# ScalarE takes ba's logits out of PSUM; block passes over 49 tiles; a folded prefix sum; one store moved

## The chip, the core and the metric

One core of a Trainium2 chip runs the whole program. Its engines are TensorE (PE; its weight loads are listed as PEld), VectorE (DVE), ScalarE (ACT), GpSimd (POOL) and SyncE (SP, which here only issues transfers). The metric is device time in microseconds (us), lower is better; the kernel before takes 11012.33 us, the median of three runs (11008.8 to 11015.49).

## What is computed

Four graph layers in a row over 6250 nodes of 128 features and 200000 edges. Cut to what matters here:

```python
# GCN: degree-normalised, weighted sum over edges
deg = segment_sum(w, dst) + 1
out = segment_sum((x @ W)[src] * norm[:, None], dst) + b
# gated graph network (2 rounds), then attention with 8 heads:
e = leaky_relu(s_i[row] + s_j[col], 0.2)
ex = exp(e - m[row])
denom = segment_sum(ex, row)                 # ba computes ex and denom
out = segment_sum(x_heads[row] * (ex / denom[row])[..., None], col)
# message passing layer, LayerNorm
```

## The kernel before

Nodes are laid out as 49 tiles of 128. The work is a row of stages, each a block with one instruction list per engine, coupled by semaphores; a barrier of all engines ends each stage. The stages that the change touches:

**prep** sorts the edges into a 49 x 49 grid of blocks (source tile by target tile), one slot per edge and at most 128 per block. Edges lie in groups of 14 x 128. A loop runs over 112 items (a group and a window of targets), two deep: GpSimd copies the item's fields, DVE makes the one-hot of the block (`OJ`), PE adds up prefix counts, DVE multiplies one-hot by prefix and reduces over 98 blocks to the edge's rank (L697 to L700), makes the one-hot of the rank (`OHr`), and PE places the records, which DVE adds into `X` (used as `RECS`). Before the loop DVE clears the buffers, `X` and `OJF` among them (L634 to L646), and then tells the others by `zeroed`. After the loop SyncE stores, in this order: `rec_d`, seven pieces of `gcn_d`, `dst2_d` (the list of edges that found no slot, by groups: `dst_d` in the trace's names), `dst2p_d` (the same by partitions), and `slot_d`, twice. `slot_d` is what the next stage reads.

**The GCN pass** (`block_pass("gcn")`) runs over target tiles, 50 of them (`NTP = NT + 1`; the last is padding, so that they go in pairs), each in 4 units of 12 or 13 blocks. SyncE loads a tile's slots (`rowsb`, two buffers), DVE makes a one-hot (L1195), PE gathers (L1267), DVE weighs (L1215) and makes the target's one-hot (L1202), PE adds (L1279), ACT copies the tile's sum out (L1254). `block_pass("heads")` does the same later, over the attention heads.

**ba** (`block_attention`) runs over 50 tiles as well, each in 3 units v of 17, 16 and 16 blocks (`AU`), two deep. In DVE's round for v stand: both one-hots of v (`hot`, L1892 and L1894); `second_rest` of v-2 (L1930); `logits` of v-1 (L1904 to L1909), which first copies PE's result `xp` from PSUM to `tx`; `source_hot` of v-1 (L1915); `first_rest` of v-1 (L1924). PE looks the logits of v up (L2012, L2015: six matmuls a block, `looks`), then adds the denominators of v-2 (L2026). ACT does, in order, `second_part` (L1973), exp (L1985), a cast (L1987), and every third unit a store. `looks` waits for `hotT` and `x_free`, DVE's `second_rest` for ACT's `part2`.

`Chain.step` makes an engine wait for its own instruction before the next. The order of the instructions is that of the code.

Of the kernel before, what the change touches and what calls it, by code (L numbers as in the profile page):

```python
# [111 lines left out]
def build(nc, x, xT, src, dst, edge_type, edge_weight, edge_attr, wpack, mats, rowpack, colpack, out):  # L112
# [43 lines left out]
    with ExitStack() as whole:  # L156
# [40 lines left out]
        wt_early = sb(early, "wt_early", [P, W_HEADS * P])  # L197
        parts = early.enter_context(ExitStack())
        FLD = sb(parts, "FLD", [P, NG, 5, GC], BF16)
        KEY0 = sb(parts, "KEY0", [P, NG * GC])  # L200
# [299 lines left out]
        with ExitStack() as ctx:  # L500
# [38 lines left out]
            d2I = KEY0[:].bitcast(I32)  # L539
# [7 lines left out]
            KEY_STEPS, RANK_STEPS, ADD_STEPS = 5, 6, 2  # L547
            STEPS = KEY_STEPS + RANK_STEPS + ADD_STEPS
            with nc.Block() as block:
                @block.sync  # L550
                def _(sp):
# [9 lines left out]
                    for c in range(NCH):  # L561
# [4 lines left out]
                    sp.dma_start(dst2_d.rearrange("g (p c) -> p g c", c=GC),  # L566
                                 d2I.rearrange("p (g c) -> p g c", c=GC)).then_inc(slots_out, 16)
# [6 lines left out]
                    sp.wait_ge(slots_out, 5 * 16)  # L574

                @block.gpsimd
                def _(pool):
                    pool.wait_ge(zeroed, 1)
# [28 lines left out]
                def _(act):  # L607
                    act.wait_ge(zeroed, 1)
                    n = act.value_load(turns_to[0:1, NCH:NCH + 1], min_val=1, max_val=KCAP // SL)
# [22 lines left out]
                def _(dve):  # L632
# [20 lines left out]
                    dve.sem_inc(place_free, 1)  # L653

# [33 lines left out]
                    def rank_hot(k, s, own, at_):  # L688
# [10 lines left out]
                        own.step(V.tensor_reduce(rank[:], prod[:], AX, ALU.add))  # L699
# [98 lines left out]
                def _(pe):  # L798
# [35 lines left out]
                    pe.wait_ge(zeroed, 1)  # L834
                    pe.matmul(prefix, zero[:], zero[:, 0:BK], start=True, stop=True)
# [274 lines left out]
        def block_pass(name, recd=None):  # L1110

            gcn = name == "gcn"
            with ExitStack() as ctx:
# [6 lines left out]
                else:  # L1120
# [14 lines left out]
                    name, "chain scaled stored part rest hotT hotD got weighed added taken back")  # L1135
                with nc.Block() as block:
                    @block.sync
                    def _(sp):
# [7 lines left out]
                        with sp.Fori(0, NTP // 2) as n:  # L1146
                            for ip in range(2):
                                sp.wait_ge(hotT, n * W2 + (ip + 1) * U)
                                sp.dma_start(rowsb[:, ip], slot_d[ds(n * 2 + ip, 1), 0].rearrange("i j r -> i (j r)").to_broadcast([P, NB])
                                             ).then_inc(rows_in[ip], 16)  # L1150
                                if not gcn:
                                    sp.wait_ge(weighed, n * W2 + (ip + 1) * U)
                                    sp.dma_start(exr[:, ip].rearrange("p b h -> p (b h)"), exb_d[ds(n * 2 + ip, 1)].rearrange("i p f -> (i p) f")
                                                 ).then_inc(ex_in[ip], 16)
                        for ip in range(2):
                            sp.wait_ge((rows_in if gcn else ex_in)[ip], 16 * (NTP // 2))
                        if gcn:
                            sp.wait_ge(hotT, NTP * U + W2)
                            sp.dma_start(tiles3(HB[:]), gcn_d.rearrange("(t p) f -> p t f", p=P)).then_inc(back, 16)
                            sp.wait_ge(hotD, NTP * U)  # L1160
                            sp.dma_start(X[:], x).then_inc(back, 16)
                            sp.wait_ge(back, 32)

                    @block.vector
                    def _(dve):
# [4 lines left out]
                        own = Chain(dve, chain)  # L1170
                        if not gcn:
# [55 lines left out]
                        def body(n, begun):  # L1227
                            for v in range(W2):
# [8 lines left out]
                        with dve.Fori(1, NTP // 2) as n:  # L1237
                            body(n, True)
                        weigh(NTP // 2 - 1, W2 - 1)

                    @block.scalar
                    def _(act):
# [9 lines left out]
                        with act.Fori(0, NTP) as i:  # L1252
# [4 lines left out]
                    def _(pe):  # L1257
# [24 lines left out]
                        def body(n, begun):  # L1282
                            for v in range(W2):
# [7 lines left out]
                        with pe.Fori(1, NTP // 2) as n:  # L1291
                            body(n, True)
                        adds(NTP // 2 - 1, W2 - 1)
# [533 lines left out]
        def block_attention(name):  # L1827

            with ExitStack() as ctx:
                ctx.callback(end_stage)  # L1830
                U, NI = len(AU), NTP // 2
# [26 lines left out]
                with nc.Block() as block:  # L1858
                    @block.sync
                    def _(sp):  # L1860
                        with sp.Fori(0, NI) as n:
                            for ip in range(2):
                                sp.wait_ge(hotT, n * W2 + (ip + 1) * U)
                                sp.dma_start(rowsb[:, ip].rearrange("p f n -> p (f n)"),
                                             slot_d[ds(n * 2 + ip, 1)].rearrange("i f j r -> i (f j r)").to_broadcast([P, 2 * NB])
                                             ).then_inc(rows_in[ip], 16)
                        for ip in range(2):
                            sp.wait_ge(rows_in[ip], 16 * NI)

                    @block.vector  # L1870
                    def _(dve):
# [25 lines left out]
                        def logits(n, v, own):  # L1897
# [35 lines left out]
                        def body(n, begun):  # L1933
                            own = Chain(dve, chain)
                            own.base = n * (W2 * 3) - (3 if begun else 0)
                            for v in range(W2):
# [9 lines left out]
                        with dve.Fori(1, NI) as n:  # L1946
                            body(n, True)
                        own = Chain(dve, chain)
# [419 lines left out]
```

## Time and profile before

| what | value |
|---|---|
| median of three runs | 11012.33 us |
| profiled execution: its own time, span | 11021.82 us, 11020.0 us |
| mean granted clock of PE | 0.726 |
| prep (with its start and end) | 106 to 1606 us |
| GCN pass | 1606 to 2603 us |
| ba | about 6970 to 7649 us |
| heads pass | about 7740 to 8723 us |
| load of a tile's slots, `HB<-slot_d` x50, issue to landing (median) | 6.2 us |

The page of the profile says, for the whole span:

```profile
PE 6146.0 (56%) x61543; PEld 5305.8 (48%) x61544; DVE 5371.8 (49%) x7184; ACT 1483.0 (13%) x4120; POOL 4858.5 (44%) x5699
```

No engine fills the span: each stage has a bound of its own, so a share of the whole says little. Three views are used below. The *timeline* has the start in us from the span's start, the duration, engine, line of the program, operation, what it writes and reads, shapes, and in brackets the idle time before it and what ended that. A *group of instructions* has the count, then busy us and mean ns of one, then idle before; a row of one *tile's* instructions has the least, middle and greatest duration in ns and the first and last start. A *sum over a stretch* has its bounds and length, the busy us of PE, PEld, DVE, ACT and POOL (with counts), the granted clock of PE as a share of full speed, the share of the transfer engines, and GB/s.

### The profile page before, as it was taken

The page shows a single profiled execution, that of the slowest core. Times are in us where ns is not written, and L with a number is a line of the kernel's source. Part 1 is how long each engine was busy: PE and PEld are TensorE (multiplying, and loading weights), DVE is VectorE, ACT ScalarE, POOL GpSimd, SP SyncE. Part 2 cuts the span into 40 slices and gives each one's busy share as a digit, 9 for nine tenths or more (in the row PEclk, how much of TensorE's full clock was granted, in tenths as well). Part 3 has the DMA queues.
Part 4 walks back from the last instruction along what each step waited for, and adds up shares of the span by engine and source line. Part 5 has one row for each costly group of instructions (what it writes and reads, how often), then busy time and mean ns, then how long its engine had stood idle before and what let it go on. Part 6 is the DMA issues. An engine that isn't in the chain of part 4 may idle for free. (4 is left out here: it accounts for less than half of the span.)

```text
span 11020.0 us, 167959 instructions
## 1 busy us (share of the span) xinstructions
PE 6146.0 (56%) x61543; PEld 5305.8 (48%) x61544; DVE 5371.8 (49%) x7184; ACT 1483.0 (13%) x4120; POOL 4858.5 (44%) x5699
## 2 busy tenths in 40 slices
PE   4666659996443343343333333576899735555554
PEld 3333339995233333333333333575899734444444
DVE  7888878885211111121212221798888643323333
ACT  3666640001100000000000000121000001111111
POOL 1111100001477777757777777001000037777775
PEclk7777769998766666666666666555999867677776
DMA  1000022222222122221111111564322112222222
GB/s 45 0 0 0 0 44 82 82 87 93 95 66 66 53 66 66 66 71 52 52 53 52 52 52 50 195 259 183 104 92 95 64 50 78 77 78 73 78 78 72
DMA packets 323571, 805.09 MB, mean 73 GB/s; under 512 B 157651, under 2 KB 196349, under 8 KB 303773
## 3 DMA queue, kind: packets, MB, share of 16 engines
q1 hardware_dynamic: 148380, 429.92, 11.4%
q0 software_dynamic: 153216, 312.49, 10.0%
q10 hardware_dynamic: 21888, 61.54, 1.4%
q8 instruction: 53, 0.87, 0.0%
q14 instruction: 34, 0.27, 0.0%
HBM read 721.60 MB, written 81.99 MB: 73 GB/s over the span
## 5 line engine op out<-in xcount | busy, mean ns | idle before, releaser
L979 POOL DMA_INDIRECT ggnn_edges_G<-trans_d,ggnn_edges_rid x3136 | 2983.9, 951 | 1229.7 <-issue 955.5
L1092 PE MATMUL ggnn_edges_PS<-ggnn_edges_OH,ggnn_edges_G 128*128 128x128 f32 x6272 | 1176.8, 373 | 2326.0 <-DMA ggnn_edges_G<-trans_d,ggnn_edges_rid 2215.6
L1092 PEld LDWEIGHTS ggnn_edges_PS<-ggnn_edges_OH,ggnn_edges_G 128*128 128x128 f32 x6272 | 1136.6, 284 | 2370.8 <-issue 2367.6
L979 POOL DMA_INDIRECT mpnn_edges_G<-msg_d,mpnn_edges_rid x1568 | 1502.8, 958 | 692.8 <-issue 473.7
L1048 DVE TENSOR_TENSOR acc<-acc,ggnn_edges_PS 128x128 f32 x224 | 64.6, 289 | 2520.4 <-PE ggnn_edges_PS L1092 2520.4
L618 ACT ACTIVATE prep_OJF<-prep_OJ,prep_fld 128x98 bf16<-128x98 bf16 x3136 | 848.9, 362 | 574.7 <-DVE prep_OJ L674 574.7
L1076 PE MATMUL mpnn_edges_PS<-wt_late,mpnn_edges_at 128*128 128x256 f32 x1568 | 544.8, 521 | 678.3 <-DVE mpnn_edges_G L1035 335.9
L1076 PEld LDWEIGHTS mpnn_edges_PS<-wt_late,mpnn_edges_at 128*128 128x128 f32 x1568 | 413.2, 271 | 790.6 <-DVE mpnn_edges_G L1035 357.1
L822 PE MATMUL prep_PS<-prep_OJF,prep_OHr 128*128 128x490 bf16 x1582 | 583.2, 551 | 225.4 <-DVE prep_OHr L701 225.4
L1035 DVE TENSOR_TENSOR mpnn_edges_G<-mpnn_edges_G,mpnn_edges_PS 128x1792 f32<-128x1792 f32 x112 | 226.3, 2021 | 875.3 <-DMA mpnn_edges_G<-msg_d,mpnn_edges_rid 691.7
L1013 DVE SCALAR_TENSOR_TENSOR ggnn_edges_OH<-dstI,ggnn_edges_itm,ggnn_edges_PS 128x896 f32<-128x896 f32 x448 | 491.6, 1144 | 228.5 <-issue 163.2
L1279 PE MATMUL gcn_GP<-gcn_hd,gcn_msg 128*128 128x128 f32 x4900 | 590.3, 277 | 0.0
L1279 PE MATMUL heads_GP<-heads_hd,heads_msg 128*128 128x128 f32 x4900 | 590.3, 277 | 0.0
L1279 PEld LDWEIGHTS gcn_GP<-gcn_hd,gcn_msg 128*128 128x128 f32 x4900 | 562.8, 192 | 0.0
L1279 PEld LDWEIGHTS heads_GP<-heads_hd,heads_msg 128*128 128x128 f32 x4900 | 562.8, 192 | 0.0
L1092 PE MATMUL mpnn_edges_PS<-mpnn_edges_OH,mpnn_edges_G 128*128 128x128 f32 x3136 | 420.0, 298 | 247.7 <-ACT mpnn_edges_G L956 247.7
L592 POOL COPY prep_dg<-dstI 128x14 int32 x112 | 26.1, 233 | 1172.4 <-PE prep_PS L831 629.5
L1092 PEld LDWEIGHTS mpnn_edges_PS<-mpnn_edges_OH,mpnn_edges_G 128*128 128x128 f32 x3136 | 415.1, 214 | 257.9 <-issue 252.9
L979 POOL DMA_INDIRECT gcn_edges_G<-gcn_d,gcn_edges_rid x28 | 30.1, 1075 | 1120.0 <-DVE gcn_edges_rid L997 1111.8
L1479 ACT ACTIVATE ggnn_edges_OH<-ggnn_edges_PS,bcol 128x896 f32<-128x896 f32 x14 | 14.1, 1007 | 3662.2 <-PE ggnn_edges_PS L1473 3662.2
L2012 PE MATMUL ba_XP<-ba_A,ba_hsT 128*128 128x16 bf16 x7350 | 408.6, 174 | 167.2 <-DVE ba_hdT L1894 162.3
L979 POOL DMA_INDIRECT gat_edges_G<-heads_d,gat_edges_rid x28 | 27.2, 972 | 1040.5 <-DVE gat_edges_rid L997 1032.3
(451 smaller groups left out, 10881.2 us busy)
## 6 DMA issues: line engine op xcount, KB each, us to landing
ba_rows<-slot_d SPq DMA_DIRECT2D x50, 3136.0 KB, 11.3
HB<-slot_d SPq DMA_DIRECT2D x50, 1568.0 KB, 6.2
heads_rows<-slot_d SPq DMA_DIRECT2D x50, 1568.0 KB, 6.2
ggnn_edges_G<-trans_d,ggnn_edges_rid POOLq DMA_INDIRECT x3136, 2.5
mpnn_edges_at<-in_edge_attr SPq DMA_DIRECT2D x112, 448.0 KB, 3.9
trans_d<-gcn_edges_tb ACTq DMA_DIRECT2D x49, 512.0 KB, 2.6
trans_d<-ggnn_edges_tb ACTq DMA_DIRECT2D x49, 512.0 KB, 3.0
mpnn_edges_G<-msg_d,mpnn_edges_rid POOLq DMA_INDIRECT x1568, 2.5
```

The costliest lines, as they stand in the source:

```text
L592: nc.gpsimd.tensor_copy(dg[:], dstI[:, ds(g * GC, GC)])
L618: ins = act.activation(OJF[:, par, c, f, :], OJ[:, par, c, :], ACT.Copy, scale=fld[:, par, f, c:c + 1])
L822: mm = pe.matmul(placed[par], OHr[:, par, c, :], OJF[:, par, c].rearrange("p f b -> p (f b)"), start=c == 0, stop=c == GC - 1)
L979: pool.indirect_dma_start(G[:, s, c, :], None, table, bass.IndirectOffsetOnAxis(ap=rid[:, s, c:c + 1].bitcast(U32), axis=0)).then_inc(gath ...
L1013: oh = V.scalar_tensor_tensor(out=OH[:, s % 2, :, a * HP:(a + 1) * HP], in0=over(dst_of[:, ds(g[s] * GC, GC)], HP), scalar=itm[:, s, 0:1], ...
L1035: V.tensor_tensor(out=ga, in0=ga, in1=ep, op=ALU.add).then_inc(summed, 1)
L1048: V.tensor_tensor(out=acc[:, ds(col, P)], in0=acc[:, ds(col, P)], in1=wp[s % 2], op=ALU.add).then_inc(added, 1)
L1076: mm = pe.matmul(ep[:, q, :], at_[:, s, q, :], W(W_M1E, 2), start=True, stop=True)
L1092: mm = pe.matmul(wp[s % 2], G[:, s, c, :], OH[:, s % 2, c, :], start=c == 0, stop=c == GC - 1)
L1279: mm = pe.matmul(accp, msg[:, par, b, :], hd[:, par, b, :], start=j == 0, stop=j == NT - 1)
L1479: act.activation(rg, gp[0], ACT.Sigmoid, bias=bcol[:, rz:rz + 1]).then_inc(gates, 1)
L2012: pe.matmul(xp[u][:, b], hsT[:, par, b, :], A3[:, first_of[u] + b, a, :], start=a == 0, stop=False, skip_group_check=True)
```

## The change

Five edits. (1) GpSimd clears `OJF` and `X`, in its own list and before `zeroed`; DVE waits for both before its loop, ACT and PE for `OJF`. (2) The reduce over 98 products becomes an add of 48 to 48, one of 24 to 24, and a reduce over 26. (3) The store of `dst2_d` moves from the end of prep to SyncE's list in the GCN pass, behind the first two loads; `KEY0`, which holds the list, lives longer for that. (4) The two block passes and ba run 24 pairs of tiles in loops as before, and the 49th tile in a body of its own instead of a 25th pair; the block passes clear the padding of `acc`. (5) In ba the copy from PSUM to `tx` moves from DVE to ACT, at the head of ACT's round.

```diff
@@ prep @@
-                    sp.dma_start(dst2_d.rearrange("g (p c) -> p g c", c=GC),
-                                 d2I.rearrange("p (g c) -> p g c", c=GC)).then_inc(slots_out, 16)
                     sp.dma_start(dst2p_d, d2I).then_inc(slots_out, 16)
...
                 def _(pool):
+                    nc.gpsimd.memset(OJF[:], 0.0).then_inc(fields_blank, 1)
+                    nc.gpsimd.memset(X[:], 0.0).then_inc(recs_blank, 1)
                     pool.wait_ge(zeroed, 1)
...
-                    own.step(V.memset(X[:], 0.0))
                     own.step(V.memset(OJ[:], 0.0))
-                    own.step(V.memset(OJF[:], 0.0))
...
+                    dve.wait_ge(fields_blank, 1)
+                    dve.wait_ge(recs_blank, 1)
...
-                        own.step(V.tensor_reduce(rank[:], prod[:], AX, ALU.add))
+                        own.step(V.tensor_tensor(out=prod[:, :, 0:48], in0=prod[:, :, 0:48], in1=prod[:, :, 50:BK], op=ALU.add))
+                        own.step(V.tensor_tensor(out=prod[:, :, 0:24], in0=prod[:, :, 0:24], in1=prod[:, :, 26:50], op=ALU.add))
+                        own.step(V.tensor_reduce(rank[:], prod[:, :, 0:26], AX, ALU.add))
@@ block_pass, SyncE @@
-                        with sp.Fori(0, NTP // 2) as n:
+                        for ip in range(2):
+                            load(0, ip)
+                        if gcn:
+                            sp.dma_start(dst2_d.rearrange("g (p c) -> p g c", c=GC),
+                                         d2I.rearrange("p (g c) -> p g c", c=GC)).then_inc(listed, 16)
+                        with sp.Fori(1, NT // 2) as n:
                             for ip in range(2):
+                                load(n, ip)
+                        load(NT // 2, 0)
@@ block_pass, DVE (PE alike) @@
+                        own.step(V.memset(acc[:, NPAD:], 0.0))
...
-                        with dve.Fori(1, NTP // 2) as n:
+                        with dve.Fori(1, NT // 2) as n:
                             body(n, True)
-                        weigh(NTP // 2 - 1, W2 - 1)
+                        body(NT // 2, True, U)
+                        weigh(NT // 2, U - 1)
@@ block_attention, DVE @@
-                            dve.wait_ge(x_ready, n * W2 + v + 3)
+                            dve.wait_ge(x_free, n * W2 + v + U + 1)
                             dve.wait_ge(exped, n * W2 + v + 1)
                             t = tx[:, 0:nb]
-                            own.step(V.tensor_copy(t, xp[u]))
-                            dve.sem_inc(x_free, 1)
@@ block_attention, ACT @@
+                                act.wait_ge(x_ready, n * W2 + v + 3)
+                                act.copy(tx[:, 0:nb], xp[u]).then_inc(x_free, 1)
                                 if v >= 1 or begun:
                                     second_part(*unit(n, v - 1))
```

What stands where, at three places. The numbers of lines differ between the two programs.

DVE in ba, one round, before (`ba_hsT` and `ba_hdT` are the one-hots, `ba_te` the logits):

```order
L1892 TENSOR_SCALAR ba_hsT<-ba_rows,iota_col 128x2048
L1894 TENSOR_SCALAR ba_hdT<-ba_rows,iota_col 128x2048
L1930 TENSOR_TENSOR ba_ex<-ba_tr,ba_ex 128x16x8
L1904 COPY ba_tx<-ba_XP 128x272
L1906 SCALAR_TENSOR_TENSOR ba_te<-ba_tx 128x136
L1908 TENSOR_TENSOR ba_te<-ba_te,ba_tx 128x136
L1909 TENSOR_SCALAR ba_te<-ba_te 128x136
L1915 TENSOR_TENSOR acc<-recS,iota1b 128x2176
L1924 TENSOR_TENSOR ba_tr<-ba_exi,ba_ex 128x136
```

In the changed program the same round has eight rows: the COPY is gone, and nothing else has moved.

ACT in ba, two rounds of the changed program (before, the rows of `ba_tx` were not there):

```order
L2003 COPY ba_tx<-ba_XP 128x272
L1996 CAST ba_ex<-ba_tr 128x16x8
L2010 ACTIVATE ba_exi<-ba_te 128x136
L2012 CAST ba_ex<-ba_exi 128x17x8
L2003 COPY ba_tx<-ba_XP 128x256
L1996 CAST ba_ex<-ba_tr 128x17x8
L2010 ACTIVATE ba_exi<-ba_te 128x128
L2012 CAST ba_ex<-ba_exi 128x16x8
```

The copy stands ahead of the second part (L1996) of the unit before, which DVE waits for.

SyncE from the end of prep into the GCN pass, before (the loads of the loop write `HB`):

```order
L563 DMA gcn_d<-HB 128x7x128 x7
L566 DMA dst_d<-KEY 128x112x14
L568 DMA dst2p_d<-KEY 128x1568
L572 DMA slot_d<-prep_OJF 49x50x128 x2
L549 UNCONDITIONAL_BRANCH
L1137 UNCONDITIONAL_BRANCH
L1146 UNCONDITIONAL_BRANCH
```

and in the changed program:

```order
L567 DMA dst2p_d<-KEY 128x1568
L571 DMA slot_d<-prep_OJF 49x50x128 x2
L550 UNCONDITIONAL_BRANCH
L1143 UNCONDITIONAL_BRANCH
L1154 DMA HB<-slot_d 128x6272 x2
L1164 DMA dst_d<-KEY 128x112x14
L1166 UNCONDITIONAL_BRANCH
```

The store of `dst_d` has moved behind the loads of tiles 0 and 1 and ahead of all others.

On GpSimd two rows are new, ahead of the loop:

```order
L575 UNCONDITIONAL_BRANCH
L577 MEMSET prep_OJF 128x13720
L578 MEMSET X 128x6272
L580 TENSOR_LOAD turns_to
L580 ISA x2
```

DVE cleared `prep_OJF` as 6860 words; here it is 13720 elements of 16 bits.

## Rows read from the trace of the kernel before

**Rows 1.** Sums over two stretches: the GCN pass and block attention (ba).

```profile
1629.00:2603.00 974.00, 971.11 (x12250) 968.64 (x12250) 812.19 (x650) 13.34 (x50) 0.00 (x0) 1.00 0.23 83
6980.00:7641.00 661.00, 492.65 (x17018) 475.73 (x17015) 618.93 (x1342) 137.31 (x448) 0.00 (x0) 0.50 0.66 248
```

**Rows 2.** Timeline of ba, one round of DVE, then PE and ACT.

```profile
7200.31 0.75 DVE L1894 TENSOR_SCALAR ba_hdT<-ba_rows,iota_col 128x2048 bf16<-128x2048 bf16 x1
7200.97 0.29 DVE L1930 TENSOR_TENSOR ba_ex<-ba_tr,ba_ex 128x136 bf16<-128x136 f32 x1
7201.18 0.42 DVE L1904 COPY ba_tx<-ba_XP 128x256 f32<-128x256 f32 x1
7201.75 0.29 DVE L1906 SCALAR_TENSOR_TENSOR ba_te<-ba_tx 128x128 f32<-128x128 f32 x1 [0.15 <-DVE ba_tx L1904]
...
7204.66 0.78 DVE L1894 TENSOR_SCALAR ba_hdT<-ba_rows,iota_col 128x2176 bf16<-128x2176 bf16 x1
...
7201.18 0.25 PE L2012 MATMUL ba_XP<-ba_A,ba_hsT 128*128 128x16 bf16 x3 [1.25 <-DVE ba_hdT L1894]
...
7203.76 0.61 PE L2026 MATMUL ba_XP<-ba_ex,acc 128*128 128x24 bf16 x17
7205.57 0.25 PE L2012 MATMUL ba_XP<-ba_A,ba_hsT 128*128 128x16 bf16 x3 [1.20 <-DVE ba_hdT L1894]
...
7208.57 0.58 PE L2026 MATMUL ba_XP<-ba_ex,acc 128*128 128x24 bf16 x16
...
7204.08 0.30 ACT L1973 CAST ba_ex<-ba_tr 128x128 bf16<-128x128 f32 x1 [0.78 <-DVE ba_tr L1924]
```

**Rows 3.** Timeline of the prep loop, DVE.

```profile
802.82 0.87 DVE L697 TENSOR_TENSOR prep_prod<-prep_OJ,prep_pfx 128x1372 bf16<-128x1372 bf16 x1 [0.15 <-DVE prep_pfx L694]
803.73 1.58 DVE L699 TENSOR_REDUCE prep_rank<-prep_prod 128x14 f32<-128x1372 bf16 x1
...
805.57 1.09 DVE L701 TENSOR_TENSOR prep_OHr<-prep_rank,prep_iob 128x1792 bf16<-128x1792 bf16 x1
```

**Rows 4.** Timeline of SyncE at prep's end, then ACT's first of the GCN pass.

```profile
1564.52 1.07 SPq L566 DMA_DIRECT2D dst_d<-KEY  x1
1565.63 24.11 SPq L568 DMA_DIRECT2D dst2p_d<-KEY  x1
1589.85 8.58 SPq L572 DMA_DIRECT2D slot_d<-prep_OJF  x2
...
1606.47 5.98 ACT L1251 CAST gcn_H<-HB 128x896 bf16<-128x896 f32 x7 [42.09 <-PEq L154]
```

**Rows 5.** Timeline of prep's start, DVE and GpSimd.

```profile
106.26 0.07 DVE L634 MEMSET prep_itm<- 128x16 int32 x1 [9.05 <-PEq L154]
...
114.49 5.29 DVE L636 MEMSET X<- 128x6272 f32 x1 [1.37 <-issue]
...
122.82 5.78 DVE L638 MEMSET prep_OJF<- 128x6860 uint32 x1 [1.50 <-issue]
...
138.30 0.20 POOL L592 COPY prep_dg<-dstI 128x14 int32 x1 [86.28 <-issue]
```

**Rows 6.** Groups of GpSimd instructions up to 140 us.

```profile
L374 POOL TENSOR_TENSOR acc<-wgt,FLD 128x1568 f32<-128x1568 f32 x1 | 3.2, 3205 | 0.1
...
L373 POOL CAST FLD<-wgt 128x1568 bf16<-128x1568 f32 x1 | 1.5, 1491 | 0.0
```

**Rows 7.** Sums over a stretch, as rows 1: the end of prep.

```profile
1568.00:1589.00 21.00, 0.00 (x0) 0.00 (x0) 0.00 (x0) 0.00 (x0) 0.00 (x0) 0.50 1.83 32
```

**Rows 8.** Instructions of tiles gcn_hsT and ba_tx.

```profile
L1195 DVE TENSOR_SCALAR gcn_hsT<-HB,iota_col x200: 611/615/649, 1628.7 to 2589.8; 128x1536 bf16<-128x1536 bf16 x100
...
L1904 DVE COPY ba_tx<-ba_XP x150: 414/418/441, 6979.6 to 7640.1; 128x256 f32<-128x256 f32 x100, 128x272 f32<-128x272 f32 x50
```

**Rows 9.** Groups of instructions: ACT copies out of PSUM.

```profile
L1254 ACT COPY acc<-gcn_GP 128x128 f32 x50 | 13.3, 267 | 963.3 <-PE gcn_GP L1279 963.3
...
L1678 ACT COPY mpnn_edges_OH<-mpnn_edges_PS 128x896 f32<-128x896 f32 x14 | 12.7, 906 | 99.6 <-PE mpnn_edges_PS L301 99.6
```

More of the change, by code:

```diff
@@ L1225, in weigh, with body @@
                                                 op=ALU.mult).then_inc(weighed, 1)
-                        def body(n, begun):
-                            for v in range(W2):
+                        def body(n, begun, units=W2):
+                            for v in range(units):
                                 hot(n, v)
@@ L1251, in _ @@
                                 act.copy(H3[:, a, at], (acc if a else HB)[:, at]).then_inc(part, 1)
-                        with act.Fori(0, NTP) as i:
+                        with act.Fori(0, NT) as i:
                             act.wait_ge(added, i * U + U + 2)
@@ L1280, in adds, with body @@
                             mm.then_inc(added, 1)
-                        def body(n, begun):
-                            for v in range(W2):
+                        def body(n, begun, units=W2):
+                            for v in range(units):
                                 fetch(n, v)
@@ L1290, in _ @@
                         body(0, False)
-                        with pe.Fori(1, NTP // 2) as n:
+                        with pe.Fori(1, NT // 2) as n:
                             body(n, True)
-                        adds(NTP // 2 - 1, W2 - 1)
+                        body(NT // 2, True, U)
+                        adds(NT // 2, U - 1)
         class Stage:
@@ L1830, in block_attention @@
                 ctx.callback(end_stage)
[L1831 removed]
+                U, NI = len(AU), NT // 2
                 W2 = 2 * U
@@ L1931, in second_rest, with body @@
                                             op=ALU.subtract).then_inc(split, 1)
-                        def body(n, begun):
+                        def body(n, begun, units=W2):
                             own = Chain(dve, chain)
-                            own.base = n * (W2 * 3) - (3 if begun else 0)
-                            for v in range(W2):
+                            own.base = n * (W2 * 2) - (2 if begun else 0)
+                            for v in range(units):
                                 hot(n, v)
@@ L1973, in second_part, with body @@
                             act.copy(ex3[:, par, 0:nb, 1], tr[:, par, 0:nb]).then_inc(part2, 1)
-                        def body(n, begun):
-                            for v in range(W2):
+                        def body(n, begun, units=W2):
+                            for v in range(units):
                                 ip, u, par = v // U, v % U, v % 2
                                 at, nb = first_of[u], AU[u]
+                                act.wait_ge(x_ready, n * W2 + v + 3)
+                                act.copy(tx[:, 0:nb], xp[u]).then_inc(x_free, 1)
                                 if v >= 1 or begun:
@@ L2029, in adds, with body @@
                             mm.then_inc(dens, 1)
-                        def body(n, begun):
-                            for v in range(W2):
+                        def body(n, begun, units=W2):
+                            for v in range(units):
                                 looks(n, v)
@@ L2039, in _ @@
                             body(n, True)
-                        adds(NI - 1, W2 - 2)
-                        adds(NI - 1, W2 - 1)
+                        body(NI, True, U)
+                        adds(NI, U - 2)
+                        adds(NI, U - 1)
                         for b in range(3):
```

66 lines of the change are left out of this document (39 added, 27 removed).

## The prediction, made before the changed kernel ran

> **What bounds the kernel now.** I read the sums over stretches first, for the engine that fills each stage the change touches; then groups of instructions for mean durations; then the timeline of one round of each loop for the distance from start to start, and SyncE's rows for the transfers. The reader should see four things.
>
> In the GCN pass PE is busy 971.11 of 974 us at a granted clock of 1.00. In block attention (ba) DVE is busy 618.93 of 661 us, ACT only 137.31, and PE, at clock 0.50, waits for DVE [rows 1, 2]. In the loop of prep DVE's instructions follow each other without a wait for another engine [rows 3]. And prep ends in a row of stores: SyncE is held 24.11 us at the issue of dst2p_d, and only then issues the slot_d stores [rows 4].
>
> The sum is made against the profiled execution, 11021.8 us (span 11020.0), which lies 9.5 us above the median of the three timed runs, 11012.3; the same difference is taken off at the end.
>
> **1. Clearing moves from DVE to GpSimd.** The memsets of X and OJF took 5.29 and 5.78 us; each also had a gap before it (1.37 and 1.50), of which about 0.9 in all goes with them [rows 5]: `zeroed` comes 12.0 us earlier, so does the load of the first item, and GpSimd's first copy could start at 126.3, not 138.30. But GpSimd first fills 13720 + 6272 = 19992 elements, from about 106.3, when the block starts. The trace has no such fill. At the pace of its one-input cast (1491 ns / 1568 = 0.95 ns) it takes 19.0 us, ends at 125.3 and hides just behind DVE and the load. At that of its two-input operation (3205 / 1568 = 2.04 ns) it takes 40.9 us, ends at 147.2, and 8.9 us are lost [rows 6]. I take the cast, the nearer row: **-12**, ends -12 and +9.
>
> The casts show 0.95 ns an element [rows 6]. The Trainium skill (GPSIMD Engine Reference, 4.1 Engine selection) calls one-input operations on this engine roughly line rate, yet its section 3.1 gives 1.96 times VectorE's time for an add and keeps elementwise work on VectorE. An estimate by that ratio from DVE's fill of X puts the end at 139.4 and turns the term into a loss of about 1, so that the sum would be 13 us smaller. The cast rows speak for the first.
>
> **2. The prefix sum is folded.** Now: one reduce over 14x98, 1.58 us, 1.62 from start to start. After: an add over 14x48 = 672 elements, one over 14x24 = 336, a reduce over 14x26 = 364. Two-input bf16 steps cost 0.87 us at 1372 and 1.09 at 1792 [rows 3], so 0.16 plus 0.52 ns an element: 0.51 and 0.33. The reduce, over the same 0.16, costs 1.04 ns an element: 0.54. With 0.04 behind each: 0.55 + 0.37 + 0.58 = 1.50. Gain 0.12 to 0.13 x 113 = **-15**; DVE is the bound, so all of it counts. Should the short rows of 48 and 24 run at the reduce's pace, the adds take 0.86 and 0.51, and the term is (0.90 + 0.55 + 0.58 - 1.62) x 113 = +46. Ends -17 and +46.
>
> **3. dst_d leaves the end of prep.** It goes in pieces of 14 words: while it runs, the core moves 32 GB/s [rows 7]. The slot_d stores are issued at 1589.85, the next pass's first work follows 16.6 us later [rows 4]. Without dst_d they are issued right behind dst2p_d, 1565.6, behind what is left of gcn_d (up to 4 us). So prep ends 20.3 to 24.2 us earlier: **-22**. In the GCN pass dst_d stands on SyncE's queue between the loads of tiles 0 and 1 and that of tile 2. The second load is in by about 1635 (first hot 1628.7 plus one load of 6.2, the page's median); 0.8 MB at 32 GB/s is 25 us, and the load of tile 2 another 6.2: 1666. Tile 2 is wanted two tiles of 19.3 us after 1628.7, at 1667. Behind it wait DVE's hot of tile 2 and then PE. Even at 26 GB/s it is late by 5. Ends 0 and +5; I take **+2**.
>
> **4. 49 tiles, not 50.** GCN pass: units start between 1628.7 and 2589.8, 961.1 / 199 = 4.83 us each, 19.3 a tile [rows 8]; the heads pass runs the same loop. PE is full, so a tile counts whole: **-19.3 twice**. ba: (7640.1 - 6979.6) / 149 = 4.43 us a unit [rows 8], three a tile: **-13.3**. The last tile's body is now code of its own. ba's mean exceeds the 4.35 of one round [rows 2] by 0.08, 12 us in all, shared by loop turns and the entry into new code: **+3** for one entry more, ends 0 and +12.
>
> **5. ba: ACT takes the logits out of PSUM.** On DVE the copy goes, with 7201.75 - 7201.18 = 0.57 us from start to start, 0.15 of it a wait for itself [rows 2]. Over 147 units that is -84 if DVE stays the bound. What is late next? ACT does copy(v) and then the second part of v-1, in order, and DVE's second rest of v-1 waits for that in its next round. From the start of one target hot: 0.75 us for the hot; 0.12 until PE starts; looks of 2.72 (7201.18 to 7203.76, and 0.14 for the last one to drain), or 3.14 for a 17-block unit (7205.57 to 7208.57) [rows 2]; ACT's copy, 0.267 us at 128 elements and 0.906 at 896, so 0.37 at 256 [rows 9], 0.30 of it before the next ACT step can begin; that step 0.30; handovers 0.14. Less the 0.66 after which the second rest stands in DVE's round [rows 2]: 0.75 + 0.12 + 2.72 + 0.74 - 0.66 = 3.67 behind a short unit, 0.78 + 0.12 + 3.14 + 0.74 - 0.66 = 4.12 behind the long one. DVE's own round is 4.35 - 0.57, about 3.75 there. So once a tile 0.38 is lost: 49 x 0.38 = 19. Term **-65**, ends -84 and 0 (the last if handovers cost 0.4 a unit more). tx has one buffer, but ACT's exp of v-1 has by then waited for DVE's last reading of it, so this adds no wait. PE needs 2.86 + 0.61 a unit, less than the new round.
>
> **Sum.** -12 - 15 - 22 + 2 - 19.3 - 19.3 - 13.3 + 3 - 65 = -161. Profiled execution: 10861. Against the median, 11012.3 - 161 = **10851 us**.
>
> **Rivals.**
> A. *DVE alone sets ba's unit.* The looks' ends are modelled, and PE's clock may rise above 0.50 as its gaps shrink. For: the overshoot is 0.38 in one unit of three, made of small handovers. Against: the chain above. Term 5 is -84: 10832 us.
> B. *The chain through PE and ACT sets it,* so that the copy was only moved. For: the chain is within 0.1 us of DVE's round already. Against: it needs 0.4 us more in each unit. Term 5 is 0: 10916 us.
> C. *The folded adds run at the slow pace.* For: no row this short in the trace. Against: the 14x98 product runs at the fast one [rows 3]. Term 2 is +46: 10912 us.
> D. *Slower: ba loses its overlap.* If the copy placed first made each unit wait for its own looks, a unit would be 1.42 hots + 0.12 + 2.86 looks + 0.37 copy + 3 x 0.29 logits + 0.60 exp and cast + 0.30 = 6.54 us, 2.11 over now: 147 x 2.11 = +310, less the other 96: 11226 us. It decides from 4.43 + 96 / 147 = 5.08 us a unit. For: one tx buffer, one ACT queue. Against: DVE works on v-1 while PE looks up v, and no wait in the diff closes that distance.
> E. *The store is only moved:* dst_d holds up the first tiles for as long as it held up the end of prep. Term 3 is 0: 10871 us.
>
> **Chances.** Forecast 0.60, A 0.17, E and smaller shortfalls of terms 1 and 3 0.10, B 0.07, C 0.03, D 0.03. The range goes from 10822 (A with the good ends of terms 2, 3 and 4) to 10892 (the forecast with terms 1, 3 and 4 at their bad ends and part of B): 2 in 10 lie outside. The likeliest case's own range is 10838 to 10872. A measurement of this kernel tells 0.2%, 22 us, from no change; all cases but D are faster by more: faster 0.96, within 0.2% 0.01, slower 0.03.
>
> **What would show it.** Term 1: GpSimd's two fills end before its first copy, near 126. Term 2: adds near 0.51 and 0.33 us. Term 3: slot_d issued right behind dst2p_d, the GCN pass's first work near 1557 (1606.5 less 27 and 22), a wait for the load of tile 2 of a few us at most. Term 4: 196, 196 and 147 units. Term 5: a ba unit of 3.95 us on average, longest behind the 17-block look-up, where DVE waits for ACT; 3.85 in all three means A, 4.4 means B. The forecast is wrong if ba stays above 4.3 us a unit, if the adds take 0.86, or if a block pass no longer runs at clock 1.00.

## The result, and the profile after

| kernel | median of four, us | range | ratio to the kernel before, 95% interval |
|---|---|---|---|
| before, beside it | 11013.91 | 11008.80 to 11018.00 | |
| changed | 10853.24 | 10841.94 to 10854.41 | 0.9851 [0.9835, 0.9867] |

The change takes off 160.7 us; forecast were 161, and a time of 10851. The profiled execution of the changed kernel is the fastest of its four, 10841.94 (span 10840.2), and its untouched stages are some 11 us shorter than in the profiled execution before. So below single stages are compared, not spans. One execution of e12, further down, took 12790.32 us at a mean granted clock of 0.635 (its others 0.68) and is left out of its median.

Sums over the three stretches that answer to [rows 1] (the GCN pass, ba, the heads pass); columns as there:

```profile
1581.00:2528.00 947.00, 945.00 (x11954) 942.57 (x11955) 794.03 (x635) 12.73 (x48) 0.00 (x0) 1.00 0.27 83
6905.00:7490.00 585.00, 485.82 (x16791) 469.32 (x16791) 550.53 (x1175) 176.17 (x589) 0.00 (x0) 0.50 0.74 278
7596.00:8542.00 946.00, 945.16 (x11960) 942.81 (x11961) 790.99 (x637) 13.51 (x49) 0.00 (x0) 1.00 0.26 90
```

PE still fills both block passes at clock 1.00; in ba DVE is busy 94%, PE 83% at clock 0.50, ACT 30%. One row each for the units of the GCN pass and of ba, with the first and last start [rows 8]:

```profile
L1213 DVE TENSOR_SCALAR gcn_hsT<-HB,iota_col x196: 610/614/649, 1581.1 to 2523.1; 128x1536 bf16<-128x1536 bf16 x147, 128x1664 bf16<-128x1664 bf16 x49
L1918 DVE TENSOR_SCALAR ba_hdT<-ba_rows,iota_col x147: 744/747/782, 6904.3 to 7483.0; 128x2048 bf16<-128x2048 bf16 x98, 128x2176 bf16<-128x2176 bf16 x49
```

(2523.1 - 1581.1) / 195 = 4.83 us a unit as before; (7483.0 - 6904.3) / 146 = 3.96 us, where it was 4.43.

The start of prep, GpSimd and DVE [rows 5]:

```profile
105.03 11.53 POOL L577 MEMSET prep_OJF<- 128x13720 bf16 x1 [53.28 <-POOLq L154]
116.49 5.32 POOL L578 MEMSET X<- 128x6272 f32 x1
126.53 0.19 POOL L593 COPY prep_dg<-dstI 128x14 int32 x1 [4.71 <-issue]
...
118.32 3.58 DVE L643 CAST prep_iob<-iota_row 128x128 bf16<-128x128 f32 x1
121.93 0.36 DVE L644 TENSOR_TENSOR prep_lower<-iota_row 128x196 f32<-128x196 f32 x1
```

GpSimd's fills take 0.84 and 0.85 ns an element and end at 121.81, 4.7 us before its first copy. But DVE's cast into `iob`, 0.23 us before, now takes 3.58, from 118.32 to 121.90, and ends with the fill. The rank steps [rows 3]:

```profile
131.98 0.94 DVE L699 TENSOR_TENSOR prep_prod<-prep_OJ,prep_pfx 128x1372 bf16<-128x1372 bf16 x1 [0.15 <-DVE prep_pfx L696]
132.95 0.51 DVE L701 TENSOR_TENSOR prep_prod<-prep_prod 128x672 bf16<-128x672 bf16 x1
133.50 0.34 DVE L702 TENSOR_TENSOR prep_prod<-prep_prod 128x336 bf16<-128x336 bf16 x1
133.87 0.53 DVE L703 TENSOR_REDUCE prep_rank<-prep_prod 128x14 f32<-128x364 bf16 x1
```

The end of prep, SyncE and ACT's first of the GCN pass [rows 4]:

```profile
1542.27 1.31 SPq L567 DMA_DIRECT2D dst2p_d<-KEY  x1
1543.69 7.66 SPq L571 DMA_DIRECT2D slot_d<-prep_OJF  x2
1574.69 0.85 SPq L1154 DMA_DIRECT2D HB<-slot_d  x2
1575.59 0.42 SPq L1164 DMA_DIRECT2D dst_d<-KEY  x1
...
1559.50 5.98 ACT L1270 CAST gcn_H<-HB 128x896 bf16<-128x896 f32 x7 [17.37 <-PEq L154]
```

slot_d is issued 1.4 us behind dst2p_d, not 24.2. And two rounds of ba, DVE, then PE, then ACT [rows 2]:

```profile
7125.38 0.78 DVE L1918 TENSOR_SCALAR ba_hdT<-ba_rows,iota_col 128x2176 bf16<-128x2176 bf16 x1
...
7129.16 0.75 DVE L1918 TENSOR_SCALAR ba_hdT<-ba_rows,iota_col 128x2048 bf16<-128x2048 bf16 x1
7130.12 0.29 DVE L1952 TENSOR_TENSOR ba_ex<-ba_tr,ba_ex 128x128 bf16<-128x128 f32 x1 [0.21 <-ACT ba_ex L1996]
...
7133.29 0.75 DVE L1918 TENSOR_SCALAR ba_hdT<-ba_rows,iota_col 128x2048 bf16<-128x2048 bf16 x1
...
7137.76 0.28 DVE L1952 TENSOR_TENSOR ba_ex<-ba_tr,ba_ex 128x128 bf16<-128x128 f32 x1
...
7126.29 0.24 PE L2038 MATMUL ba_XP<-ba_A,ba_hsT 128*128 128x16 bf16 x3 [0.66 <-DVE ba_hdT L1918]
...
7134.16 0.25 PE L2038 MATMUL ba_XP<-ba_A,ba_hsT 128*128 128x16 bf16 x3 [0.97 <-DVE ba_hdT L1918]
...
7129.50 0.39 ACT L2003 COPY ba_tx<-ba_XP 128x272 f32<-128x272 f32 x1 [1.55 <-PE ba_XP L2041]
7129.78 0.30 ACT L1996 CAST ba_ex<-ba_tr 128x128 bf16<-128x128 f32 x1
...
7136.92 0.37 ACT L2003 COPY ba_tx<-ba_XP 128x256 f32<-128x256 f32 x1 [1.22 <-PE ba_XP L2041]
7137.19 0.30 ACT L1996 CAST ba_ex<-ba_tr 128x128 bf16<-128x128 f32 x1
```

Behind the 17-block look-up (PE from 7126.29, ACT's copy at 7129.50) DVE's second rest waits 0.21 us for ACT: 7129.16 to 7133.29 is 4.13 us. Behind the short look-up ACT's cast ends at 7137.49 and DVE needs it at 7137.76: no wait.

### The profile page after: what moved, and what is told of

It reads as the page before. It is cut to its first block and busy times, and to the rows that moved or that the text cites. A ratio compares the mean times of both kernels' runs of the same rounds, so it can differ in the third digit from the quotient of the medians.

```text
span 10840.2 us, 166167 instructions
## 1 busy us (share of the span) xinstructions
PE 6085.7 (56%) x60710; PEld 5246.5 (48%) x60711; DVE 5239.4 (48%) x7210; ACT 1520.1 (14%) x4256; POOL 4873.9 (45%) x5701
## 5 line engine op out<-in xcount | busy, mean ns | idle before, releaser
L826 PEld LDWEIGHTS prep_PS<-prep_OJF,prep_OHr 128*128 128x128 bf16 x1582 | 205.5, 136 | 549.0 <-issue 347.2
```

The lines of the kernel that those rows point to most:

```text
L826: mm = pe.matmul(placed[par], OHr[:, par, c, :], OJF[:, par, c].rearrange("p f b -> p (f b)"), start=c == 0, stop=c == GC - 1)
```

## The experiments

The first four ran together, with a median of 11015.47 for the kernel before beside them, so their medians stand against 10853.24. In e5 to e12 every kernel took 1690 to 1760 us more, the one before too (12768, 12771 and 12708 beside them). Where that lies is seen in sums over the stages ggnn (the gated graph network) and mpnn (the message passing layer), first of the changed kernel in its first run, then in e11, the same kernel:

```profile
2801.00:6852.00 4051.00, 1501.82 (x7145) 1315.99 (x7145) 799.60 (x1117) 104.33 (x105) 2975.26 (x3136) 0.65 0.20 58
8790.00:10834.00 2044.00, 1019.72 (x5096) 893.05 (x5096) 686.76 (x760) 218.12 (x154) 1500.15 (x1568) 0.71 0.26 77
```

```profile
2811.00:7906.00 5095.00, 1583.13 (x7147) 1278.10 (x7147) 787.93 (x1116) 104.33 (x105) 2968.11 (x3136) 0.59 0.17 46
9843.00:12600.00 2757.00, 1132.67 (x5096) 958.61 (x5096) 693.03 (x761) 218.14 (x154) 1482.95 (x1568) 0.64 0.21 57
```

The same 3136 and 1568 instructions that gather rows from memory keep GpSimd busy as long, but the data arrive more slowly (46 for 58 GB/s, 57 for 77), and these two stages scatter by tens of us from run to run (ggnn by 45 us and mpnn by 54 over the traces of e5 to e12). All other stages last within a few us of what they did. So e5 to e12 are judged by the stage that they change, in their traces; their totals can only fail to contradict that.

**e1. The copy back on DVE.**

```diff
-  act.wait_ge(x_ready, n * W2 + v + 3)
-  act.copy(tx[:, 0:nb], xp[u]).then_inc(x_free, 1)
...
+  own.step(V.tensor_copy(t, xp[u]))        # DVE, in logits
+  dve.sem_inc(x_free, 1)
```

> Undoes term 5 alone: in block attention DVE copies the looked-up logits out of PSUM again and ACT does not; everything else is as in the changed kernel. Chain theory (the forecast's: with the copy on ACT a short unit follows DVE at about 3.8 us and the one behind the 17-block look-up waits for PE and ACT at 4.10): a unit goes back from 3.96 to 4.43 us, 147 x 0.47 = +69 us against the changed kernel, so about 10922. DVE-only theory (each of the 147 units gained the whole 0.57 us of the copy): +84, about 10937. If much of the 82 us that the stage lost came from elsewhere (the missing tile is 13 of it): +50 or less.

Measured: 10921.15 us (10917.07 to 10925.13), ratio 0.9915 [0.9899, 0.9932], +67.9. In the trace a unit takes 4.427 us (first target hot at 6911.5, 147th at 7557.9). The chain theory gave +69, DVE alone +84: the chain.

**e2. ACT's second part before the copy.**

```diff
-  act.wait_ge(x_ready, n * W2 + v + 3)
-  act.copy(tx[:, 0:nb], xp[u]).then_inc(x_free, 1)
   ...                                       # second_part(v - 1)
+  act.wait_ge(x_ready, n * W2 + v + 3)
+  act.copy(tx[:, 0:nb], xp[u]).then_inc(x_free, 1)
```

> In the changed kernel ACT copies the logits of unit v and then does the second part of unit v-1. Here the second part of v-1 comes first. Chain theory: DVE's second rest of v-1 no longer stands behind PE's look-ups of v and ACT's copy; the unit behind the 17-block look-up falls from 4.10 to about 3.8 us, 49 x 0.3 = -15 us against the changed kernel, about 10838. DVE-only theory (DVE alone sets each unit and the 0.3 us is something of its own, such as its longer row): no change, within 3 us. Third: ACT then waits for DVE's exp input first and starts the copy later, which would show as a wait of DVE in front of its logits step and cost up to +15.

Measured: 10842.49 (10839.18 to 10846.07), ratio 0.9843 [0.9826, 0.9859], -10.7. The chain theory gave -15, DVE alone nothing. The unit behind the long look-up fell from 4.10 to 3.825 us (medians over 49), the others stayed at 3.77 and 3.78. ACT's rows, the cast now ahead of the copy and right behind DVE:

```profile
7125.57 0.30 ACT L1996 CAST ba_ex<-ba_tr 128x128 bf16<-128x128 f32 x1 [0.72 <-DVE ba_tr L1946]
7126.43 0.39 ACT L2005 COPY ba_tx<-ba_XP 128x272 f32<-128x272 f32 x1 [0.56 <-PE ba_XP L2041]
```

49 x 0.276 = 13.5 would be the gain of that wait; 10.4 came over 147 units. The rest: in the first dozen units PE is late for other reasons (in the changed kernel its rows there wait 13.2 us at "issue"), and DVE then stands at the next step that needs it (12.1 us ahead of its logits step in all, against 2.1, and 9.6 of the 12.1 in that dozen). From the 13th unit on 10.0 us were gained.

**e4. The copy twice.**

```diff
+  act.copy(tz[:, 0:nb], xp[u])
   act.copy(tx[:, 0:nb], xp[u]).then_inc(x_free, 1)
```

> ACT copies the looked-up logits twice: first into a scratch tile that nobody reads, then as in the changed kernel. About 0.3 to 0.37 us more between PE's look-ups and DVE's logits step and ACT's second part, none of it on DVE; ACT stays below half busy. Chain theory: the long unit takes all of it (4.10 to 4.4, 49 x 0.3 = 15 us), the short ones, 0.1 us of slack by the forecast's sum (3.67 against 3.75), take 0.2 (98 x 0.2 = 20 us): +35 us, about 10888. DVE-only theory: no change, within 3 us.

Measured: 10865.17 (10864.00 to 10865.77), ratio 0.9863 [0.9847, 0.9879], +11.9: neither the chain's +35 nor DVE's nothing. By kind of unit the medians are 3.80, 4.355 and 3.79 (3.77, 4.10, 3.79 in the changed kernel). The long one took 0.25 of the 0.28 by which ACT's next step moved, as the chain says; the short ones took 0.03 and nothing. One row of ba each, of the changed kernel, of e2 and of e4: DVE's second rest, with its idle time before it.

```profile
L1952 DVE TENSOR_TENSOR ba_ex<-ba_tr,ba_ex 128x136 bf16<-128x136 f32 x147 | 42.5, 289 | 17.8 <-ACT ba_ex L1996 17.8
```

```profile
L1952 DVE TENSOR_TENSOR ba_ex<-ba_tr,ba_ex 128x136 bf16<-128x136 f32 x147 | 42.5, 289 | 0.7 <-ACT ba_ex L1996 0.7
```

```profile
L1953 DVE TENSOR_TENSOR ba_ex<-ba_tr,ba_ex 128x136 bf16<-128x136 f32 x147 | 43.1, 293 | 31.0 <-ACT ba_ex L1997 31.0
```

The wait for ACT goes from 17.8 to 0.7 with the order turned, and to 31.0 with a longer chain. That DVE alone sets the unit is out.

**e3. The store back in prep.**

```diff
+  sp.dma_start(dst2_d..., d2I...).then_inc(slots_out, 16)     # end of prep
...
-  sp.dma_start(dst2_d..., d2I...).then_inc(listed, 16)        # GCN pass
```

> Puts the store of dst2 (dst_d, the overflow list) back among the stores at the end of prep. Forecast's theory (it holds up the end of prep by 20 to 25 us, and beside the GCN pass it costs only a short wait for the load of tile 2, 1.7 us): +24 us against the changed kernel, about 10877. Rival E (the transfer is only moved and holds up the GCN pass as long): within 3 us of the changed kernel. In the trace the GCN pass's first work should come about 25 us later behind the last step of the prefix loop, and the distance from unit 7 to unit 8 be 4.83 us.

Measured: 10877.90 (10874.66 to 10879.40), ratio 0.9874 [0.9858, 0.9891], +24.7. SyncE's rows show the wait return to dst2p_d, behind dst_d:

```profile
1546.41 1.28 SPq L567 DMA_DIRECT2D dst_d<-KEY  x1
1547.73 27.74 SPq L569 DMA_DIRECT2D dst2p_d<-KEY  x1
1575.58 8.32 SPq L573 DMA_DIRECT2D slot_d<-prep_OJF  x2
```

The GCN pass begins 89.3 us behind the last item's first step (60.3 in the changed kernel, 58.5 to 61.0 in all others that move the store), and PE runs through its 196 units without a wait, 940.4 us. Rival E, that the transfer is only moved, is out. SyncE is held 27.74 us at dst2p_d here and 24.11 in the kernel before, so this way back is some 3 us longer than the way there. That both terms were sized rightly isn't shown by this: see e9 and e11.

**e5. Clearing back on DVE.**

```diff
-  nc.gpsimd.memset(OJF[:], 0.0).then_inc(fields_blank, 1)
-  nc.gpsimd.memset(X[:], 0.0).then_inc(recs_blank, 1)
...
+  own.step(V.memset(X[:], 0.0))
...
+  own.step(V.memset(OJF[:], 0.0))
```

> Puts the clearing of X and OJF (memsets) back on DVE at the start of prep. Forecast's theory (DVE is what the first item waits for, GpSimd's fills are hidden): +11 to +12 us against the changed kernel, all of it before the first item. Rival (the fills on GpSimd only move the wait, since a DVE cast stood still for 3.4 us while they ran): +11 less 3.4, so +8, if that cast is quick again once GpSimd has nothing to do; then the cast into iob should take about 0.25 us, as in the kernel before (0.23), where it took 3.58 in the changed one.

Measured: 12616.46 us in the slower surroundings (e11 12606.23). From DVE's first memset to the first item's one-hot 34.68 us, against 24.08 to 24.11 in the traces that keep the change and the cast: 10.6 us. The cast into `iob` is short again, as the rival had it:

```profile
133.31 0.23 DVE L642 CAST prep_iob<-iota_row 128x128 bf16<-128x128 f32 x1
```

Why not the rival's +8: it took 3.4 from 11, but the memsets and their gaps come to 13.9 (e7), less 3.3. The loop behind is a little faster than in the changed kernel: 12.330 us an item for 12.342 to 12.359, 2.4 us in all (see term 2 below). From the first memset to the GCN pass e5 takes 8.3 us more than e11, not 10.6.

**e7. The cast as a maximum of two inputs.**

```diff
-  own.step(V.tensor_copy(iob[:], iota_row[:]))
+  own.step(V.tensor_tensor(out=iob[:], in0=iota_row[:], in1=iota_row[:], op=ALU.max))
```

> In the changed kernel DVE's cast of iota_row into iob took 3.58 us, 118.32 to 121.90, while GpSimd filled X (116.49 to 121.81); in the kernel before it took 0.23. Here the same values are written by a two-input operation (the maximum of iota_row with itself). Theory P (a one-input DVE copy that runs in its fast form cannot start while GpSimd fills memory, a two-input one can; a two-input step beside the same fill was not held): the step takes about 0.25 us and the step in which prep's tables are done comes 3.3 us earlier; the kernel's time falls by 3 at most, less if the load is late next. Theory Q (any DVE operation at that place is held, for its data or for the row it reads): 3.6 us again, no change.

Measured: 12594.50 us. The rows, beside GpSimd's fill of X:

```profile
118.60 5.32 POOL L578 MEMSET X<- 128x6272 f32 x1
125.36 0.19 POOL L593 COPY prep_dg<-dstI 128x14 int32 x1 [1.44 <-issue]
...
120.43 0.29 DVE L643 TENSOR_TENSOR prep_iob<-iota_row 128x128 bf16<-128x128 f32 x1
...
129.07 0.17 DVE L671 TENSOR_SCALAR prep_win<-prep_off 128x14 int32<-128x14 int32 x1 [7.76 <-issue]
```

0.29 us for 3.58, with the fill under way all the while: theory P. GpSimd's first copy comes 3.3 us earlier after the stage's start, the first one-hot only 1.8 (22.30 us for 24.09): DVE then stands at "issue", 1.6 us behind GpSimd's last field.

**e6. The fold taken back.**

```diff
-  own.step(V.tensor_tensor(out=prod[:, :, 0:48], in0=prod[:, :, 0:48], in1=prod[:, :, 50:BK], op=ALU.add))
-  own.step(V.tensor_tensor(out=prod[:, :, 0:24], in0=prod[:, :, 0:24], in1=prod[:, :, 26:50], op=ALU.add))
-  own.step(V.tensor_reduce(rank[:], prod[:, :, 0:26], AX, ALU.add))
+  own.step(V.tensor_reduce(rank[:], prod[:], AX, ALU.add))
```

> Takes the fold back: one reduce over 14x98 in place of two adds and a reduce over 14x26, in every one of the items' rank steps. Forecast: +15 us (0.13 x 113). By the two traces: an item went from 12.43 to 12.34 us, so +9.5 us (0.086 x 111), with the three instructions 0.14 shorter where they stand and 0.05 given back in later steps of the item. Rival: the difference per item is noise and the fold is worth nothing: within 3 us.

Measured: 12615.78 us. An item takes 12.442 us, against 12.342 to 12.359 in the traces with the fold and GpSimd's clearing (12.352 in e11): 0.09 an item, 10 us in all. The fold is worth two thirds of its forecast.

**e8. All 50 tiles.**

```diff
-  with dve.Fori(1, NT // 2) as n:
+  with dve.Fori(1, NTP // 2) as n:        # likewise on each engine, in both passes and ba
```

> Both block passes and block attention go over all 50 tiles again, in 25 pairs and with no last tile of its own; everything else as in the changed kernel. Forecast's sizes, a block pass at 4.83 us a unit and attention at 3.96: +19.3 + 19.3 + 11.9 = +50.5 us, less 0 to 3 for the entry into the last tile's own code; +48 to +50, so about 10903. Rival (a tile's end is hidden beside the next stage's start): +30 or less.

Measured: 12654.51 us, +48.3 to e11 by the medians. By stages, from first work to the next stage's: GCN pass 1014.6 against 992.6 (+22.0, of which 2.6 is the store's higher cost in the first two tiles), heads +19.5, ba 618.0 against 605.6 (+12.4). A tile of ba at 3.97 is 11.9: the entry into the last tile's own code costs nothing that can be seen.

**e9. The store two loads later.**

```diff
+  for ip in range(2):
+      load(1, ip)
   sp.dma_start(dst2_d..., d2I...).then_inc(listed, 16)
-  with sp.Fori(1, NT // 2) as n:
+  with sp.Fori(2, NT // 2) as n:
```

> Only the place of the dst_d store changes: SyncE issues it behind the loads of tiles 2 and 3 of the GCN pass, not behind those of tiles 0 and 1. In the traces with the store at its place in the changed kernel, PE stands 1.2 to 5.8 us at 'issue' in its second tile (a transfer on the instruction queue is under way among the store's small packets then) and tile 2's load comes late by 2 to 5 us: 196 units from first to last hot took 942.0 us in the changed kernel's profile and 946.9 to 947.7 in others, and 940.4 with the store back in prep. Theory (both waits belong to the store, and by the time of the third and fourth tile the loop's code is in and tile 4's load has room): first to last hot 940 to 941, so 2 to 7 us faster than the changed kernel, about 10848. Rival (the store delays whatever load or code comes next, wherever it stands): 942 to 948 again, no change.

**e11. The changed kernel again.** No edit.

> The changed kernel once more, unaltered, beside the two others and on the same chip: what these two gain is read against this run. Both theories: 10853 within 4 us of its first median if the chip gives the same clocks, and 0.985 of the kernel before in any case. Its first profiled execution waited 1.7 us in the GCN pass for tile 2's load where four others waited 6 to 8: here first to last hot of the 196 units should be 946 to 948, not 942, if that first one was the exception.

Measured: e9 12605.40, e11 12606.23 us (12572.53 to 12636.48), ratios 0.9873 both, so the totals tell nothing. First to last hot of the 196 units: 946.4 us in e11, 943.8 in e9. e11 is as expected, and the first profile was the exception: with the store at its place in the changed kernel, eight traces of 196 units gave 942.0 once and 946.4 to 948.1 otherwise, against 940.4 without it (e3). e9 lies between its two theories, and needs its tiles looked at. The second tile, from its first hot to the third tile's, took 19.36 us in all traces without the store there (before, e3, e9, e10, e12), 21.0 in the changed kernel's first trace and 24.2 to 27.5 in the eight others with it. The first tile varies by 1.2 us with the store or without (15.8 in e3, 17.0 in e9 and before), as PE's granted clock there does (mean 0.88 in e3, 0.81 in e9). So the store costs the pass 5 to 8 us, once 1.6, all of it in the second tile. What waits is not what I named. e11's rows of PE in the second tile, and the transfer queues in three stretches around (packets, MB, share of 16 engines):

```profile
1606.52 1.79 PE L1286 MATMUL gcn_GP<-gcn_H,gcn_hsT 128*128 128x128 bf16 x29 [1.62 <-issue]
1619.57 1.57 PE L1286 MATMUL gcn_GP<-gcn_H,gcn_hsT 128*128 128x128 bf16 x25 [2.94 <-issue]
```

```profile
q1 hardware_dynamic: 4566, 0.26, 190.8%
q8 instruction: 1, 0.02, 1.5%
...
q1 hardware_dynamic: 329, 1.42, 92.4%
q8 instruction: 1, 0.02, 2.0%
...
q1 hardware_dynamic: 169, 1.72, 22.9%
q8 instruction: 3, 0.05, 1.0%
```

PE stands in the middle of a unit, with its one-hot there, at "issue". The stretches are 1595 to 1605, 1616 to 1622 and 1622 to 1640. In e9 one such wait is left, 2.0 us, in the fourth tile (0.6 and none in e10 and e12, which store at the same place): the second pair of tiles is the loop's first turn.

The wait is not the whole price. In seven of the nine traces the granted clock fell after such a wait, the first in e1, e6 and e8, the second in e2, e4, e5 and e7. The second tile of e3, then that of e1, where PE had stood 3.3 us at "issue" and is then busy 22.4 us for the same work.

```profile
1629.22:1648.59 19.37, 19.37 (x250) 19.32 (x246) 16.26 (x15) 0.27 (x1) 0.00 (x0) 1.00 0.28 106
```

```profile
1596.79:1622.47 25.68, 22.39 (x248) 22.05 (x246) 16.34 (x14) 0.27 (x1) 0.00 (x0) 0.87 1.43 117
```

In those seven the tile's mean clock is 0.87 to 0.94 and PE is busy 21.2 to 22.4 us; in the changed kernel's first trace (1.2 us of wait) and in e11 (4.6) it stayed at 1.00. Why not in e11, the traces don't tell.

**e10 and e12. All three.** The swap of e2, the maximum of e7 and the later store of e9, in one kernel, run twice.

> Three edits together: ACT's second part of v-1 before its copy of v in block attention (measured alone at -10.7 us), iob by the two-input maximum in place of the cast (1.8 us earlier to the first item in its trace), and the dst_d store behind the loads of tiles 2 and 3 (expected -2 to -7). They lie in different stages, so they should add: -14 to -19 us against the changed kernel, about 10837, and about -177 against the kernel before. If the gains overlap or the later store has a price of its own: -11 or less.

> The three edits together once more, unaltered, since the chip of the last comparison took some 1750 us more for either kernel in the stages of the message-passing gathers and scattered by 60 us there. If this chip is like the first one: by the stages of the last trace (22.4 us from the first memset to the first item's work against 24.2, 941.3 us of GCN pass against 946.4, 568.1 us of block attention against 579.1) 18 us less than the changed kernel, about 10835 against 10853, ratio to the kernel before 0.984. If the gains are given back in later stages: 10845 to 10853, ratio 0.985. On a chip like the last one the total tells nothing and only the stages do.

Measured: 12599.00 and 12548.85 us, ratios 0.9878 [0.9853, 0.9903] and 0.9880 [0.9860, 0.9900]. e11, run beside e10 alone, gave 0.9873 [0.9848, 0.9898]: by the total no gain is shown. By stages, e10 and e12 against e11: start of prep 22.3 us both for 24.1; GCN pass, first to last hot, 941.3 and 940.6 for 946.4; ba, first to last, 568.1 and 568.9 for 579.1. That is 17.9 and 17.8 us, within the 14 to 19 expected; 1.0 of it is the first tile, which was slow in e11 (16.9 us for 15.9 and 16.0). The part that e2 measured in full stands; the other 7 are shown in their stages only.

## Why the prediction was right

The total is right, and by its own steps. That it is right to 0.3 us is luck: errors of 10 us either way cancelled.

| term | forecast | runs |
|---|---|---|
| 1 clearing | -12 | -10.6 (e5) |
| 2 fold | -15 | -10 (e6) |
| 3 store, end of prep | -22 | -25.6 (85.9 to 60.3 us from the last item to the GCN pass) |
| 3 store, GCN pass | +2 | +5 to +8 (e3, e11) |
| 4 tile, two passes | -19.3 each | -19.4, -19.5 (e8) |
| 4 and 5, ba as a stage | -75.3 | -81.8 (686.8 to 605.0 us) |

With 6.5 for the store the right column gives -10.6 - 10 - 25.6 + 6.5 - 19.4 - 19.5 - 81.8 = -160.4, against -160.7 measured. Clearing, fold and the store in the pass came out 10.9 us worse than forecast, the end of prep, the tiles and ba 10.4 better. Nor is the column itself good to 0.3: its rows are read from single traces, and where e3 put the whole of term 3 back it cost 24.7 us, not 25.6 - 6.5 = 19.1.

*Term 1.* The cast rate was the right end: 0.84 ns against the 0.95 taken. What the term missed is that DVE's own cast would stand still during the fill. Without that hold the tables are done 13.9 us earlier (e7), with it 10.6; at the first item's one-hot it is 12.4 and 10.6, so the forecast's 12 was right but for 1.8 us of the hold. The Trainium skill (SBUF — State Buffer, Who interferes with whom) says that a DVE copy or cast in a two-port mode and GpSimd lock each other out, whoever is first, and that a DVE instruction with two inputs contends with one that reads on GpSimd, not with one that only writes. Cast 3.58, maximum 0.29 beside the same fill: the traces agree; a GpSimd instruction that reads, beside a DVE one with two inputs, no run here shows. By that rule the hold of 3.3 us could have been foreseen.

*Term 2.* Durations were as forecast (0.51, 0.34, 0.53). From the first of them to the step behind the last a folded item takes 1.51 us and an unfolded one 1.62 (means in e11 and e6); the forecast had 1.50. So 0.11 is gained where the steps stand, not 0.13, and 0.02 of it is given back in the mean: in every fourth item DVE stands 0.13 us ahead of its one-hot, not 0.04. All eleven traces that have both the fold and GpSimd's clearing show this, and none of the others: not the kernel before, not e6 (no fold), and not e5, which folds but clears on DVE. So the fold alone gave 0.10 to 0.11 an item (12.330 in e5; 12.429 before and 12.442 in e6), 11 to 12 us, and the two edits together give 2.4 back. Why, the runs don't tell. Half of what the term fell short by is in its own sum (0.11 for 0.13), the other half in the step that DVE is the bound, so that all of it counts.

*Term 3.* The stores' queue behaved as read. The load of tile 2 cost 0.20 us in the changed kernel's trace and nothing elsewhere; the price of the move is PE's wait at "issue", a term that the prediction didn't have, and mostly outside the end of +5 that it gave. In seven traces of nine 2 to 3 us of it are a granted clock that fell behind the wait.

*Term 4.* Whole tiles at the pass's own pace; the +3 for new code was not needed (e8).

*Term 5.* The long unit came at 4.10 where the chain gave 4.12. e1 puts the copy at 67.9. The stage gained 6.5 more than terms 4 and 5 together, half of it the 3 for new code. Part of the rest is a slip: 4.35 - 0.57 is 3.78, not the 3.75 used, and with it a tile loses 0.34 and the term is -67. What the forecast had wrong inside is the slack of the short units: it made the chain 3.67 and DVE's round 3.75. In the rows, from the hot at 7133.29 the chain is through at 7137.49 + 0.04, so 4.24 - 0.66 = 3.58, against 3.77. And the short unit behind a delayed one has 0.2 more. That is why e4, sized with 0.1 of slack, was three times too high.

*Rivals.* A (DVE alone) and B (copy only moved) fell with e1, e2 and e4; C with the rows of the fold; D with 3.96 us a unit; E with e3.

## What to carry to other kernels

When a step goes from the bound engine to one that is 20% busy, trace the new chain unit by unit and compare it with the bound engine's shortened round: here 49 of 147 units were longer, and turning two steps of the helping engine's order gave 10.7 us back, free. A store of many tiny packets is cheap where nobody waits at its end, but whatever else uses the transfer engines then can come late (here, as inferred, PE's code), and the pause can cost PE clock as well (seven traces of nine here). Before clearing moves to GpSimd, look which DVE steps run beside it.

## What had not been expected of the hardware

- A DVE cast of 128 elements took 3.58 us beside a GpSimd memset, 0.23 alone; the same as a two-input maximum took 0.29 beside it.
- GpSimd's memset took 0.84 ns an element in bf16 (13720 in 11.53 us) and 0.85 in f32 (6272 in 5.32).
- PE stood at "issue" for 1.2 to 5.8 us in all in the second tile while a store of small packets was under way or just done, in all nine traces with the store at that place, and not at all there in the five others. In seven of the nine its granted clock then fell (mean over the tile 0.87 to 0.94).
- The stages of the gathers lasted 5095 and 2757 us in one run of the changed kernel and 4051 and 2044 in another, with GpSimd as busy in both; the granted clock of PE there was 0.59 and 0.65 in the first of the two stages. Why, these runs don't tell.
